# Layer one's attention: the maximum taken on VectorE before the exponential, three tiles ahead, and one exponential on ScalarE in place of two

## What is computed

```python
alpha_src = jnp.einsum('nhc,hc->nh', xl, a_src)
alpha_dst = jnp.einsum('nhc,hc->nh', xl, a_dst)
e = jax.nn.leaky_relu(alpha_src[src] + alpha_dst[dst], 0.2)
m = jax.ops.segment_max(e, dst, num_segments=n)
e = jnp.exp(e - m[dst])
s = jax.ops.segment_sum(e, dst, num_segments=n)
alpha = e / (s[dst] + 1e-16)
out = jax.ops.segment_sum(xl[src] * alpha[:, :, None], dst, num_segments=n)
```

## Time and profile before

| | |
|---|---|
| median of the runs | 1024.36 us |
| lowest and highest run | 1019.54 and 1024.40 us |
| the profiled execution, device time | 1019.75 us |
| its span | 1017.9 us |
| mean granted TensorE clock | 0.940 |
| layer one's attention, first to last matmul | 479.9 to about 697.3 us of the span |

### The profile page before, as it was taken

How to read it: one execution, slowest core, us unless ns; L and a number is a source line. 1 busy time by engine, 2 the same in 40 slices (tenths; PEclk the granted TensorE clock), 3 DMA queues, 4 the chain that set the end, 5 groups by cost and what they waited for, 6 DMA issues and landing times.

```text
span 1017.9 us, 13650 instructions
## 1 busy us (share of the span) xinstructions
PE 862.4 (85%) x4888; PEld 544.8 (54%) x4888; DVE 733.8 (72%) x1182; ACT 312.7 (31%) x535; POOL 90.4 (9%) x92
## 2 busy tenths in 40 slices
PE   2799888889889989965999967879998989899781
PEld 2455555455555434422888856756555556455440
DVE  6678777778756668894677788785966542588887
ACT  0332322241002011113677655661122000444430
POOL 4000000100100003441000000001110000000001
PEclk9799999989999999987999989979999999899796
DMA  7000000213231012313230023110122624101112
GB/s 257 1 1 2 1 2 1 99 43 122 87 157 42 27 60 91 134 62 97 76 99 26 26 68 93 52 37 21 42 93 87 256 82 156 63 1 62 62 62 89
DMA packets 22611, 72.26 MB, mean 71 GB/s; under 512 B 2595, under 2 KB 3339, under 8 KB 22303
## 3 DMA queue, kind: packets, MB, share of 16 engines
q1 hardware_dynamic: 20030, 61.01, 17.3%
q0 software_dynamic: 2528, 10.55, 3.1%
HBM read 51.22 MB, written 20.33 MB: 70 GB/s over the span
## 4 chain that ended last, share of the span: by engine, by line
PE 29%; issue 25%; DVE 20%; POOL 3%; ACT 2%; DMA 2%; POOLq 0%; DVEq 0%; ACTq 0%; SPq 0%
PE psum L796 11%; PE psum L615 9%; PE psum L769 8%; DVE arena L1173 7%; DVE arena L1274 2%; DVE arena L1278 2%; DVE arena L1141 1%; DVE arena L1183 1%; DVE arena L1297 1%; POOL arena L567 1%; ACT arena L929 1%; DMA arena<-as_scratch 1%; DVE arena L1305 1%; POOL arena L539 1%; ACT arena L941 1%
## 5 line engine op out<-in xcount | busy, mean ns | idle before, releaser
L615 PE MATMUL psum<-arena 128*128 128x512 f16 (+1 forms) x1080 | 228.9, 370 | 8.1 <-DVE arena L999 7.1
L796 PE MATMUL psum<-arena 128*128 128x257 f32 x800 | 184.9, 393 | 34.0 <-ACT arena L929 24.4
L861 ACT ACTIVATE arena<-psum 128x320 f16<-128x320 f32 (+5 forms) x140 | 83.0, 626 | 378.7 <-PE psum L615 120.7
L796 PEld LDWEIGHTS psum<-arena 128*128 128x128 f32 x800 | 156.7, 197 | 60.9 <-issue 26.1
L615 PEld LDWEIGHTS psum<-arena 128*128 128x128 f16 (+1 forms) x1080 | 105.4, 100 | 117.0 <-issue 8.8
L769 PE MATMUL psum<-arena 128*128 128x512 f16 x960 | 160.6, 330 | 2.4 <-ACT arena L929 2.4
L769 PEld LDWEIGHTS psum<-arena 128*128 128x128 f16 x960 | 94.9, 99 | 66.2 <-issue 2.9
L941 ACT ACTIVATE arena<-arena 128x640 f32<-128x640 f32 x160 | 119.6, 829 | 8.2 <-DVE arena L1278 7.0
L836 PE MATMUL psum<-arena 128*128 128x512 f16 x600 | 106.3, 341 | 15.0 <-DVE arena L1376 14.8
L861 ACT ACTIVATE arena<-arena 128x256 f16<-128x256 f32 (+2 forms) x84 | 50.5, 614 | 157.1 <-DVE arena L1387 74.3
L1173 DVE CUSTOM_DVE_ANT_0 arena<-arena 128x1280 bf16<-128x1280 bf16 x50 | 88.2, 1825 | 13.1 <-DMA arena<-as_scratch 13.1
(11 more groups left out here) (157 smaller groups left out, 625.8 us busy)
## 6 DMA issues: line engine op xcount, KB each, us to landing
arena<-in_L_gnn_W_dram SPq DMA_DIRECT2D x14, 384.0 KB, 5.6
r_scratch<-arena SPq DMA_DIRECT2D x10, 512.0 KB, 2.6
arena<-uv_scratch SPq DMA_DIRECT2D x16, 320.0 KB, 3.9
arena<-r_scratch SPq DMA_DIRECT2D x10, 512.0 KB, 3.7
x_scratch<-arena SPq DMA_DIRECT2D x10, 384.0 KB, 4.7
arena<-x_scratch SPq DMA_DIRECT2D x10, 384.0 KB, 3.5
r_scratch<-arena SPq DMA_DIRECT2D x10, 384.0 KB, 2.6
arena<-r_scratch SPq DMA_DIRECT2D x10, 384.0 KB, 4.0
```

Of the source, the lines that this page charges most:

```text
L615: ins = pe.matmul(o[:, a:b], part[:, k, ds(t * P, P)], w[:, k, a:b], start=(k == 0 and n == 0 and m == 0), stop=(k == kn - 1 and n == 1))
L796: last = pe.matmul(p_att[:, j, 0:HID + 1], pf[n % PSLOTS][:, j * P:(j + 1) * P], xl[ch % H][:, k, 0:HID + 1], start=(k == 0), stop=(k == T ...
L861: act.activation(out_, in_, ACT.Copy, scale=scale).then_inc(signal, 1)
```

## The change

For each tile VectorE now takes the larger exponent, not the larger exponential. Since `as_8` holds 0.8 times the source term, `max(u + as_8, v)` is the larger exponent less `0.2 a_src`, which ScalarE adds as its bias in the one exponential it applies, in place. VectorE's step is one `scalar_tensor_tensor` (add, max) with a pointer scalar, done three tiles ahead of the tile whose weights it makes. The six slots `ez` lie where the three plus three slots lay. The wait for the rows goes from ScalarE to VectorE, and the rows are freed as the first exponent of the next chunk is taken, where they were freed after the last weights of the old. Three exponents stand ahead of the first tile. `as_8` is made once, beside `as_s`.

```diff
 ESLOTS = 3
+ZSLOTS, Z_AHEAD = 6, 3
...
-        e1 = [at(79 * KB + 2560 * i, [W1C], f32) for i in range(ESLOTS)]
-        e2 = [at(86 * KB + 512 + 2560 * i, [W1C], f32) for i in range(ESLOTS)]
+        ez = [at(79 * KB + 2560 * i, [W1C], f32) for i in range(ZSLOTS)]
...
-                if k == 0:
-                    act.wait_ge(S[f"uvr{ch % 2}"], (ch // 2 + 1) * 32)
-                if n >= ESLOTS:
-                    act.wait_ge(S["pf_ok"], n - ESLOTS + 1)
-                for e, row, a in ((e1, uv_row[ch % 2][0], asd), (e2, uv_row[ch % 2][1], as_s)):
-                    act.activation(e[s], row, ACT.Exp, bias=a[:, ch % H, k:k + 1]).then_inc(S["ex_ok"], 1)
+                act.wait_ge(S["z_ok"], n + 1)
+                act.activation(ez[s], ez[s], ACT.Exp, bias=as_s[:, ch % H, k:k + 1]).then_inc(S["ex_ok"], 1)
...
-            dve.wait_ge(S["dve"], steps_done(1))
+            dve.tensor_scalar(as_8, asd[:, 0:H, :], 1 - SLOPE, None, ALU.mult).then_inc(S["dve"], 1)
+            dve.wait_ge(S["dve"], steps_done(2))
...
+            def exponents(n):
+
+                ch, k, s = n // T, n % T, n % ZSLOTS
+                if k == 0:
+                    dve.wait_ge(S[f"uvr{ch % 2}"], (ch // 2 + 1) * 32)
+                    if ch:
+                        dve.wait_ge(S["z_ok"], n)
+                        dve.sem_inc(S["uv_free"], 1)
+                if n >= ZSLOTS:
+                    dve.wait_ge(S["pf_ok"], n - ZSLOTS + 1)
+                u_row, v_row = uv_row[ch % 2]
+                dve.scalar_tensor_tensor(ez[s], u_row, as_8[:, ch % H, k:k + 1], v_row, ALU.add, ALU.max).then_inc(S["z_ok"], 1)
...
-                dve.wait_ge(S["ex_ok"], n * 2 + 2)
-                dve.tensor_tensor(e1[s], e1[s], e2[s], ALU.max).then_inc(S["g_ok"], 1)
+                if n + Z_AHEAD < 2 * H * T:
+                    exponents(n + Z_AHEAD)
                 if n >= PSLOTS:
                     dve.wait_ge(S["p_free"], n - PSLOTS + 1)
-                dve.wait_ge(S["g_ok"], n + 1)
-                dve.scalar_tensor_tensor(pf[n % PSLOTS], e1[s], 1.0, CT[:, k, ds(ch // H * W1C, W1C)],
+                dve.wait_ge(S["ex_ok"], n + 1)
+                dve.scalar_tensor_tensor(pf[n % PSLOTS], ez[s], 1.0, CT[:, k, ds(ch // H * W1C, W1C)],
                                          ALU.min, ALU.mult).then_inc(S["pf_ok"], 1)
-                if k == T - 1:
-                    dve.wait_ge(S["pf_ok"], n + 1)
-                    dve.sem_inc(S["uv_free"], 1)
...
+            for n in range(Z_AHEAD):
+                exponents(n)
             for n in range(H * T):
                 make_weights(n)
```

More of the change, by code:

```diff
@@ L255, in gnn_program @@
         r2_ld = [at(107 * KB, [D], f32), at(110 * KB, [D], f32)]
+        as_8 = asd_w[:, H:2 * H, :]
         asd2 = asd[:, 0:2, :].rearrange("p a t -> p (a t)")
@@ L298, in gnn_program @@
             xl_done xl_read xl_ones r1_done r1_read r1_sb r1_out0 r1_out1 neg_out
-            uv_free uv_ok uv_tr uv_rows uv_dram uvr0 uvr1 ex_ok g_ok pf_ok p_free rsum_ok att_read
+            uv_free uv_ok uv_tr uv_rows uv_dram uvr0 uvr1 z_ok ex_ok pf_ok p_free rsum_ok att_read
             ln_var ln_rstd h1_ok h1_tr h1t_hi_ok h1t_lo_ok r_in0 r_in1
@@ L932, in exps @@
             def exps(n):
-                ch, k, s = n // T, n % T, n % ESLOTS
+                ch, k, s = n // T, n % T, n % ZSLOTS
                 if k == EVICT_AT and ch:
                     evict(ch - 1)
-                if k == 0:
-                    act.wait_ge(S[f"uvr{ch % 2}"], (ch // 2 + 1) * 32)
-                if n >= ESLOTS:
-                    act.wait_ge(S["pf_ok"], n - ESLOTS + 1)
-                for e, row, a in ((e1, uv_row[ch % 2][0], asd), (e2, uv_row[ch % 2][1], as_s)):
-                    act.activation(e[s], row, ACT.Exp, bias=a[:, ch % H, k:k + 1]).then_inc(S["ex_ok"], 1)
+                act.wait_ge(S["z_ok"], n + 1)
+                act.activation(ez[s], ez[s], ACT.Exp, bias=as_s[:, ch % H, k:k + 1]).then_inc(S["ex_ok"], 1)
             for n in range(H * T):
```

## The result

| | before | changed |
|---|---|---|
| median of the runs | 1023.39 us (1019.54 to 1024.40) | 1009.80 us (1008.89 to 1010.61) |
| ratio, 95% interval | | 0.9874 (0.9845 to 0.9902) |
| profiled execution | 1019.75 us | 1010.26 us |
| its span | 1017.9 us | 1008.5 us |
| mean granted clock | 0.940 | 0.941 |

The change is worth 1.3% by the runs and 9.4 us of span between the two profiled executions. A second comparison gave 1011.08 us and 0.9878 (0.9861 to 0.9896). In the changed kernel the exponent is line 1277, the exponential line 938, the weights line 1289, the eviction line 930, `sums` lines 1260 and 1264, the matmuls line 797.

What follows compares the result with a forecast made beforehand. TensorE was taken to bound the attention's first half, VectorE's stream the second; 9.1 us there plus 0.8 at the start made 9.9: 1009.9 from the profiled execution, 1014.5 from the median, middle 1012, range 1005 to 1019 us.

Steps and rivals of the forecast that it cites:

- What bounds each half: Attention: TensorE bounds chunks 0 to 3; VectorE's own stream is the path from tile 43 to the last `sums`.
- The turn: Ahead of tiles 43, 53 and 63: eviction to first weights falls from 4.32 to 2.62 us, saving 5.1 us in all.
- The pair: VectorE's exponent and weights, no longer dependent: 1.54 against 1.68 us a tile; 0.135 us saved in 26 tiles, 3.5 us.
- Freeing the rows: Once a chunk VectorE waits for its own last result; three such places on the path, 0.5 us saved.
- the stall behind the weight load: ScalarE waits 9.05 us for a weight load, VectorE idles 2.36 us behind it; moves earlier, not shortened.
- The new wait for rows: In VectorE's stream three tiles ahead of a chunk; rows asked for seven tiles ahead of need; cost 0.
- The start: First matmul 0.8 us earlier if GpSimd's addition holds the first weights; 2.4 us if they run freely.
- A free dependence: Waiting for the VectorE instruction just before costs nothing, so only 5.1 us gained: 1014.7 to 1019.3 us; chance 7%.
- TensorE taking the path back: TensorE may be last at the middle turns; about 3 us less gain, 1012.9 to 1017.5 us; chance 10%.
- The exponent was not slow: Rival: VectorE's exponent with pointer scalar at half pace, about 1.55 us, losing 20 us: 1030 us; chance 4%.
- the rows were never late: Rival: a late row load holds a chunk's last three tiles; one chunk 5 us late, 1014.9 to 1019.5; chance 3%.
- the rival that other waits stand behind those for ScalarE: VectorE's waits for ScalarE are followed by another, such as a weight load at each turn; 1017 to 1024; chance 4%.

Runs made afterwards that it cites:

- the last experiments: Two edits of the changed kernel: `sums` ahead of the fifth layer norm's start, 1007.38 us; casts of next weights 5 and 6 moved to tiles 74 and 75, 1006.46 us.

## Why the prediction was right, point by point

The forecast took 9.9 us from the profiled execution. The traces show 9.4, or 10.4 without the microsecond by which the stage began later. The median fell further, by 13.6 and 12.6 us, for the reason left open above; the forecast of 1012 lies 2 us over it. 1012 was the middle between 1009.9 and 1014.5, not the result of a sum, so that part of its nearness is luck: what is borne out is the 9.9 us between profiled executions.

What bounds each half. Right. From the first matmul to the eviction of chunk 3 nothing was gained (92.73 and 93.03 us; the 0.30 us are the first 100 records, 23.30 and 23.60) though VectorE and ScalarE were relieved. In the second half VectorE's stream was the path: what left it came back one for one in the last experiments (2.80 for 2.81, 4.32 for 4.2 us).

The turn, 3 x 1.70 = 5.1 us. Right in mechanism, a little too large: 4.32 became 2.76, 1.56 us each, 4.7 in all. The missing term is the hand-off from ScalarE to VectorE: the first weights start 0.96 us after the exponential's start, and the sum had its duration alone, 0.83. Of the 1.56 us the second exponential is 0.71, shown by putting it back (3.47 against 2.76 us); the rest is line 1274 and its dependence, which no longer stand between.

The pair, 26 x 0.135 = 3.5 us. Right: by the medians of the stretch 1.67 became 1.53, and the exponent 0.875 us as forecast from line 1289 of the kernel before. Its two halves were measured apart. The dependence costs 0.23 us a pair in this kernel, more than the 0.18 read from the earlier trace rows; the pointer scalar 0.06 us, and 1.4 us in the stretch. Together they would make 0.17 us and not 0.14; the rest is open.

Freeing the rows, 0.5 us, and the stall behind the weight load. The waits behind tiles 49, 59 and 69 are gone. From the start of line 1278 to the next step of VectorE were 0.98, 1.06 and 1.05 us there, where 0.74 are usual: 0.9 us in all, more than the 0.5 of the forecast, which took the idle time alone. No run measured them by themselves. One of them in the kernel before:

```profile
625.04 1.28 DVE L1297 SCALAR_TENSOR_TENSOR arena<-arena 128x1024 f32<-128x1024 f32 x1 [0.24 <-DVE arena L1278]
```

The stall stayed as it was forecast:

```profile
648.13 0.84 ACT L862 ACTIVATE arena<-arena 128x768 f16<-128x768 f32 x1 [11.28 <-DMA arena<-in_L_gnn_W_dram]
...
649.92 1.23 DVE L1313 TENSOR_TENSOR arena<-psum,arena 128x1024 f16<-128x1024 f32 x1 [2.52 <-ACT arena L862]
```

2.52 us where the earlier trace rows had 2.36, the difference being what the tile before it gained. Together the terms were 9.1 us; the stretch shows 9.46. Read from the traces they are 4.7, 3.6 (26 x 0.14) and 0.9, and 0.3 come from a wait for an exponential right behind the stall in the kernel before, for which the sum had no term: 9.5 us.

The new wait for rows. Cost 0, right: it occurs once, 6.58 us at the start, where VectorE was idle anyway.

The start, 0.8 us. Right: 0.86 to the first matmul. The bound was chosen by the row of line 1274, and cutting the addition short showed that choice right. But the forecast said that the first matmuls run at the low clock "whichever it is". That was wrong: with the addition away they run at full clock, and the free start is worth 3.2 us, not 1.6.

`as_8`: no cost. The copy behind it still waits 0.35 us for TensorE's transpose.

The rivals. A free dependence is refuted by putting the wait back. TensorE taking the path back did not happen: in chunks 5 and 6 it had to wait for the eviction at each turn. The exponent was not slow, the rows were never late. Of the rival that other waits stand behind those for ScalarE, only the stall of 2.52 us is there, which the forecast had counted. A slower outcome had nothing in the traces.

## What to carry to other kernels

Find the stretch in which an engine's own stream is the path, and count only what leaves that stream there. 80 of ScalarE's exponentials were worth 2.3 us in it, and one wait for the instruction just before, on VectorE in 26 tiles, nearly 6. Where VectorE allows it, don't put two instructions side by side of which the second waits for the first. In a chain from VectorE over ScalarE back to VectorE one tile of distance was enough, and none at all cost 47 us. After such a change look again at what still stands ahead of the turns and of the start: moving two things behind the last turn and one away from the start gave another 12.6 us.

## What the runs showed of the hardware that was not expected

- A wait for the VectorE instruction just before costs 0.2 us: 1.02 us from start to start against 0.79 at the same duration of 0.88.
- The granted clock after a gap doesn't follow from the gap's length alone. After 2.78 us at the start it was 1.00 (479 to 483 us in the kernel with the short addition). After 2.87 us, at the changed kernel's turn to chunk 6, the 30 records that follow take 8.43 us where full pace is 6.6, and the granted clock is 0.59 from 629.8 to 634. After 6.74 us the last chunk's start is low too:

```profile
663.00:668.00 5.00, 5.00 (x13) 3.96 (x14) 3.06 (x3) 4.86 (x8) 0.00 (x0) 0.52 0.01 2
```

- GpSimd's addition took 2.35 us where VectorE stood idle as it began, and held the VectorE step that came behind it for 1.5 us. Begun while VectorE's two-input steps were running, it took 3.60 us, and the exponent behind them 2.98 in place of 0.88.
